# Scores of twelve heads as 64-row matmuls of two heads, and one scale transfer for each weight piece

## The reference

```python
x = x + xattn(layernorm(x), ctx)      # x: (2, 2048, 512), ctx: (2, 77, 512)
x = x + ffn(layernorm(x))             # 512 -> 1408 -> 512
# xattn: 16 heads of 32
q, k, v = heads(a @ Wq.T + bq), heads(ctx @ Wk.T + bk), heads(ctx @ Wv.T + bv)
s = einsum('bhtd,bhsd->bhts', q, k) / sqrt(32) + causal   # -inf above the diagonal
out = merge(einsum('bhts,bhsd->bhtd', softmax(s), v)) @ Wo.T + bo
# ffn: every operand rounded to fp4 in blocks of 16 along the last axis, with a scale per block
gate, y = fp4(x) @ fp4(w_gate).T, fp4(x) @ fp4(w_up).T
return fp4(silu(gate) * y) @ fp4(w_down).T
```

## Time and profile before

| | us |
|---|---|
| median of 3 runs | 1179.66 |
| lowest and highest run | 1179.59, 1182.97 |
| span of the profiled execution, first to last instruction | 1176.7 |
| PE busy | 1158.8 |
| VectorE busy | 970.3 |
| ScalarE busy | 483.5 |
| POOL busy | 179.3 |

### The profile page before, as it was taken

One profiled execution on the slowest core, in us unless ns is written; L12 is line 12 of the kernel. 1 busy time (PEld: TensorE's weight loads), 2 busy tenths in 40 slices (PEclk: granted clock), 3 DMA queues, 4 the chain that ended last, 5 costly groups with the idle time before them and its releaser, 6 DMA issues.

```text
span 1176.7 us, 21716 instructions
## 1 busy us (share of the span) xinstructions
PE 1158.8 (98%) x6784; PEld 1057.6 (90%) x6784; DVE 970.3 (82%) x1609; ACT 483.5 (41%) x1201; POOL 179.3 (15%) x305
## 2 busy tenths in 40 slices
PE   7899999999999999999999999999999999999998
PEld 6688888888888889999999999999999999999997
DVE  6778888888888877988888888888888888888865
ACT  3556656566566553333332332233233323333321
POOL 3433333333333310000000000000000000000000
PEclk9999999999999999999999999999999999999999
DMA  7223323323344436554445345444534454453442
GB/s 240 45 89 88 111 88 110 91 84 111 108 139 148 132 108 194 150 105 86 89 89 102 70 93 99 88 88 87 105 70 93 98 90 88 82 104 76 82 85 46
DMA packets 154955, 119.30 MB, mean 101 GB/s; under 512 B 95597, under 2 KB 122301, under 8 KB 154660
## 3 DMA queue, kind: packets, MB, share of 16 engines
q1 hardware_dynamic: 154916, 118.85, 42.7%
HBM read 74.47 MB, written 24.94 MB: 84 GB/s over the span
## 4 chain that ended last, share of the span: by engine, by line
PE 78%; SPq 7%; DMA 7%; DVE 2%; ACT 2%; issue 2%; POOL 2%; POOLq 0%; DVEq 0%; ACTq 0%
PE g_ps L175 7%; PE u_ps L175 7%; PE u_ps L176 7%; PE g_ps L176 7%; PE u_ps L177 7%; PE g_ps L177 7%; PE d_ps L1436 6%; PE d_ps L1437 6%; PE d_ps L1435 6%; SPq L504 4%; DMA ws_dram<-w_rows 4%; PE o_ps L784 3%; PE s_ps L764 3%; DMA w_wide<-ws_dram 3%; POOL w_q L586 2%
## 5 line engine op out<-in xcount | busy, mean ns | idle before, releaser
L175 PE MATMUL g_ps<-wguh,xnh 128*128 128x352 f32 x496 | 162.4, 327 | 0.5 <-issue 0.5
L175 PE MATMUL u_ps<-wguh,xnh 128*128 128x352 f32 x496 | 159.9, 322 | 0.5 <-DVE hid L1576 0.5
L176 PE MATMUL u_ps<-wgul,xnh 128*128 128x352 f32 x496 | 159.8, 322 | 0.0
L176 PE MATMUL g_ps<-wgul,xnh 128*128 128x352 f32 x496 | 159.8, 322 | 0.0
L177 PE MATMUL u_ps<-wguh,xnl 128*128 128x352 f32 x496 | 159.6, 322 | 0.0
L177 PE MATMUL g_ps<-wguh,xnl 128*128 128x352 f32 x496 | 159.5, 322 | 0.0
L898 ACT ACTIVATE probs<-s_ps,nsmax 128x77 f32<-128x77 f32 x512 | 113.7, 374 | 92.2 <-DVE nsmax L990 92.2
L1576 DVE TENSOR_TENSOR hid<-u_ps,silu 128x352 f32<-128x352 f32 x128 | 66.8, 522 | 78.1 <-PE u_ps L177 75.8
L1437 PE MATMUL d_ps<-wd,hql 128*128 128x512 f32 x330 | 128.9, 391 | 0.0
L1436 PE MATMUL d_ps<-wd,hqh 128*128 128x512 f32 x330 | 128.9, 391 | 0.0
L1435 PE MATMUL d_ps<-wd,hqh 128*128 128x512 f32 x330 | 128.4, 389 | 0.0
(11 more groups left out here) (175 smaller groups left out, 2547.1 us busy)
## 6 DMA issues: line engine op xcount, KB each, us to landing
scale_wide<-st_dram SPq DMA_DIRECT2D x248, 88.0 KB, 3.4
xin<-in_x_dram SPq DMA_DIRECT2D x32, 256.0 KB, 2.8
x_dram<-x SPq DMA_DIRECT2D x32, 256.0 KB, 2.2
xin<-x_dram SPq DMA_DIRECT2D x32, 256.0 KB, 2.7
out_dram<-y SPq DMA_DIRECT2D x32, 256.0 KB, 2.1
scale_wide<-st_dram SPq DMA_DIRECT2D x248, 32.0 KB, 1.8
w_wide<-ws_dram SPq DMA_DIRECT2D x240, 32.0 KB, 1.9
wd_dram<-wd_out SPq DMA_DIRECT2D x11, 512.0 KB, 3.0
```

What stands on the lines that cost most here:

```text
L175: pe.matmul(out, lh, rh, start=(i == 0), stop=False)
L176: pe.matmul(out, lh, rl, start=False, stop=False)
```

## The change

Heads 0 to 11 are computed two at a time. For each chunk `c` of 0 to 2 there are two calls: the lower 64 rows (heads 4c and 4c+1) write 154 columns of bank 0, the upper 64 rows (heads 4c+2 and 4c+3) write 154 columns of bank 1. Heads 12 to 15 stay one call of 128 rows into bank 2. So bank 0 holds heads 0, 1, 4, 5, 8, 9 and bank 1 holds 2, 3, 6, 7, 10, 11 (`S_ORDER`), and ScalarE writes each head's exponentials to its old place in `probs`. `s_done` for banks 0 and 1 is raised in the last round.

For the weight pieces, `grid_t` gets two buffers, and its transpose waits for POOL's product two pieces back. The scales lie in `ws_dram` as (8, 4, 128) instead of (4, 8, 128), and one DMA loads them to all 128 partitions. In SP's list the load of the next piece moves behind `scales_out` and `scales_in`.

```diff
+PAIR = 2 * CTX
-S_PARTS = [(0, 0, 4), (1, 4, 6), (1, 6, 8), (2, 8, 12), (3, 12, 16)]
+S_ORDER = [[4 * c + 2 * r + j for c in range(3) for j in range(2)] for r in range(2)] + [[12, 13, 14, 15]]
...
-        grid_t = sb("grid_t", [P, EC, P], BF16)
-        w_rows, w_wide = sb("w_rows", [E // BLK, P]), sb("w_wide", [P, EC, P])
+        grid_t = sb("grid_t", [P, 2, EC, P], BF16)
+        w_rows, w_wide = sb("w_rows", [E // BLK, P]), sb("w_wide", [P, EC * P])
...
             def scales_out(n):
                 sp.wait_ge(w_rows_ready, n - BY_DMA + 1)
                 if n > BY_DMA:
-                    sp.wait_ge(w_wide_loaded, 16 * (P // BLK) * (n - BY_DMA))
-                sp.dma_start(ws_dram.rearrange("c b k -> (c b) k"), w_rows[:]).then_inc(w_rows_stored, 16)
+                    sp.wait_ge(w_wide_loaded, 16 * (n - BY_DMA))
+                sp.dma_start(ws_dram.rearrange("b c k -> c b k"), w_rows[:]).then_inc(w_rows_stored, 16)
...
             def scales_in(n):
                 sp.wait_ge(w_rows_stored, 16 * (n - BY_DMA + 1))
                 if n > BY_DMA:
                     sp.wait_ge(wq_ready, n)
-                for b in range(P // BLK):
-                    sp.dma_start(w_wide[b * BLK:(b + 1) * BLK, :, :],
-                                 ws_dram[:, b, :].unsqueeze(0).to_broadcast([BLK, EC, P])).then_inc(w_wide_loaded, 16)
+                sp.dma_start(w_wide[:], ws_dram.rearrange("b c k -> b (c k)").unsqueeze(1).to_broadcast(
+                    [P // BLK, BLK, EC * P])).then_inc(w_wide_loaded, 16)
+
+            def grid_transposed(n):
+                sp.wait_ge(wquant.grid_ready, n + 1)
+                if n - 2 >= BY_DMA:
+                    sp.wait_ge(wq_ready, n - 1)
+                sp.dma_start_transpose(grid_t[:, n % 2], wquant.magic[:]).then_inc(grid_t_loaded, 16)
...
-                if n + 1 < PIECES:
-                    load_piece(n + 1)
                 if by_dma(n - 1):
                     scales_out(n - 1)
                     scales_in(n - 1)
+                if n + 1 < PIECES:
+                    load_piece(n + 1)
...
-                for i, (c, h0, h1) in enumerate(S_PARTS):
-                    bank, o = h0 // S_HEADS, (h0 % S_HEADS) * CTX
-                    out = s_ps[:, bank, o:o + (h1 - h0) * CTX]
+                def masked(out, heads):
                     if causal:
-                        pe.matmul(out, ident16[:], mask[:].unsqueeze(1).to_broadcast([P, h1 - h0, CTX]),
-                                  start=True, stop=False)
-                    last = pe.matmul(out, qt[:, c, :], kbd[:, b, c, (h0 % 4) * CTX:(h0 % 4 + h1 - h0) * CTX],
-                                     start=not causal, stop=True)
-                    if i in (1, 3, 4):
-                        last.then_inc(s_done, 1)
+                        pe.matmul(out, ident16[:], mask[:].unsqueeze(1).to_broadcast([P, heads, CTX]), start=True, stop=False)
+
+                for c in range(3):
+                    pairs = [s_ps[:, half, c * PAIR:(c + 1) * PAIR] for half in range(2)]
+                    for half in range(2):
+                        masked(pairs[half], 2)
+                    for half in range(2):
+                        r = slice(64 * half, 64 * (half + 1))
+                        last = pe.matmul(pairs[half], qt[r, c, :], kbd[r, b, c, half * PAIR:(half + 1) * PAIR],
+                                         start=not causal, stop=True)
+                        if c == 2:
+                            last.then_inc(s_done, 1)
+                masked(s_ps[:, 2, 0:4 * CTX], 4)
+                pe.matmul(s_ps[:, 2, 0:4 * CTX], qt[:, 3, :], kbd[:, b, 3, :],
+                          start=not causal, stop=True).then_inc(s_done, 1)
...
-    ws_dram = nc.dram_tensor("ws_dram", (EC, P // BLK, P), F32, kind="Internal").ap()
+    ws_dram = nc.dram_tensor("ws_dram", (P // BLK, EC, P), F32, kind="Internal").ap()
```

More of the change, by code:

```diff
@@ L583, in scale_turned @@
                 pool.wait_ge(grid_t_loaded, 16 * (n - BY_DMA + 1))
-                pool.wait_ge(w_wide_loaded, 16 * (P // BLK) * (n - BY_DMA + 1))
+                pool.wait_ge(w_wide_loaded, 16 * (n - BY_DMA + 1))
                 pool.wait_ge(wl_ready, n)
-                pool.tensor_tensor(w_q[:].rearrange("p (c k) -> p c k", k=P), grid_t[:], w_wide[:],
-                                   ALU.mult).then_inc(wq_ready, 1)
+                pool.tensor_tensor(w_q[:].rearrange("p (c k) -> p c k", k=P), grid_t[:, n % 2],
+                                   w_wide[:].rearrange("p (c k) -> p c k", k=P), ALU.mult).then_inc(wq_ready, 1)
             def iteration(a, n, down=None):
@@ L894, in exps @@
                     act.wait_ge(nsmax_ready, S_BANKS * t + bank + 1)
[L895 to L899, removed]
+                    for i, h in enumerate(S_ORDER[bank]):
+                        at = bank * S_HEADS + i
+                        last = act.activation(probs[:, h * CTX:(h + 1) * CTX], s_ps[:, bank, i * CTX:(i + 1) * CTX], ACT.Exp,
+                                              bias=nsmax[:, at:at + 1], scale=1.0)
                     last.then_inc(probs_ready, 1)
```

## The result

| | before | after |
|---|---|---|
| median of the runs | 1181.14 us (4 runs) | 1174.32 us (4 runs, 1171.94 to 1174.96) |
| span of the profiled execution | 1176.7 us | 1172.9 us |
| scores of tile 1 to scores of tile 31 | 371.02 us | 362.91 us |
| scores of tile 31 to the end | 757.6 us | 760.2 us |

The ratio is 0.9939 with a 95% interval of 0.9924 to 0.9954, so the changed kernel is about 7.2 us faster. 1174.1 us was forecast. The four rows above already tell that the agreement is not as clean as the number: the tiles in the third row gained 8.1 us where 6.2 were forecast for them (29 tiles of 0.24 us less, one masked tile of 0.8 us more), and the work behind them lost 2.6 us where nothing was.

What follows compares the result with a forecast made beforehand. PE was taken to bound attention, the weight loop close behind. Score savings of -7.2 us and +1.6 for masked tiles gave -5.6: span 1176.7 to 1171.1, plus 2.96 outside it, 1174.1 us; range 1159 to 1192.

Steps and rivals of the forecast that it cites:

- What bounds the kernel: Attention: PE sets the pace at 12.33 us a tile; the weight-piece loop, 12.45 us a piece, is close behind.
- Overlap: Six two-head score calls: the array's halves work fully side by side, 7 slots of 0.131 us, 0.92 us.
- rival 1: Score block: half-height loads go one after the other, block 2.25 us, total 1186.6 us, slower; chance 0.20.
- rival 2: Score block: no overlap at all, block 2.49 us, 1194 us, or 1180 with free shape changes; chance 0.15.
- Changes of shape: Entering and leaving the 64-row shape on PE costs 0.20 us each, twice a tile, 0.40 us.
- rival 4: Score block: changes of shape are free, total 1160 us; chance 0.52 shared with the forecast and its neighbours.
- Masked tiles: Tiles 0 and 16: three rounds, each entered and left, block 3.53 us, +0.8 us each, +1.6 for two.
- "No cost" for the path through the exponentials: From scores through exponentials to the probabilities' transposes: allows a tile every 11.2 us, under the 12.09 forecast, so no cost.
- The weight pieces: Weight loop: one scale load and a second buffer bring 12.45 to 10.0 us or less; worth nothing alone.
- Rival 3: Weight loop: single load lands late, loop stays 12.45 us, PE waits, about 1180 us; chance 0.08 with other no-change ways.
- The tail at 0: End of attention: PE's 1.3 us wait for VectorE's att stays; bounds 0 and -1.3 us, 0 taken.
- The sum: Whole kernel: -7.2 us for 30 tiles and +1.6 for the masked two make -5.6 us.

Runs made afterwards that it cites:

- the wait filled: Changed kernel plus 16 transposes that nobody reads, in PE's wait for VectorE's last attention results; 1171.26 us, ratio 0.9907.

## Why the prediction came out right

The mechanism and the sign were right; the number was helped by misses that cancel, and that it agrees to 0.2 us is luck. By the prediction's own steps:

- **What bounds the kernel.** Right. PE set the pace, and the weight loop, 0.12 us a tile slower, stood just behind: with the scores alone it came out at once (12.59 us a tile). "A granted clock of 2.4 GHz throughout" was wrong for the set-up (0.66 from 12 to 16 us); nothing in the sum hung on it.
- **Overlap.** Right in kind, mis-sized: "a call's second matmul waits for its first" gave seven slots, 0.92 us; measured are six pairs, 6 x 0.131 = 0.79 us. The two instructions of a call do not keep the halves apart; each half runs its own six in turn. The speedup table of the Trainium skill (TensorEngine Tiling (Array Packing), Theoretical Speedup), up to 2x for 64 rows, is met in full: 12 x 0.131 = 1.57 us became 0.79. The loads of the two halves run side by side as well (187 ns each, twelve of them within 0.82 us), which put an end to rival 1 and rival 2. The Trainium skill (TensorEngine Tiling (Array Packing), Key Properties) states that different tiles can execute loads and matmuls in parallel, and this trace agrees. (A 64-row load takes 187 ns, a 128-row one of the four-head call 189, as the Trainium skill's rule beside rival 1 had it; but since the loads of the halves run beside each other nothing is paid for that.)
- **Changes of shape.** Right: 0.40 us was taken, and the rows give 0.39. The distance from the projection's last matmul to the first score went from 0.23 to 0.32 us (0.09 of drain), the first pair's distance is 0.235 instead of 0.131 (0.104 of exposed load), and leaving the shape adds about 0.095 and 0.105. One row of the set-up and the idle-engine row had carried that. Together: 1.61 + 0.09 = 1.70 us, for 1.84 forecast. Two changes more cost 0.20 each again, so rival 4 is out.
- **Masked tiles.** Mis-sized: +0.8 us each was forecast, +0.07 measured. A round of masks and scores takes 0.71 us (231.70 to 232.41) where the prediction's parts make 0.95: two slots instead of three, and changes of shape that cost about 0.06 less each beside short mask matmuls.
- **"No cost" for the path through the exponentials.** This step failed. I took it as exponentials, transposes of the probabilities, 11.2 us a tile. The loop that counts goes on from the exponentials over four ScalarE steps to VectorE and takes 12.07 us; its rows were there in the trace of before, stretched to PE's 12.33 by slack too short to be marked (ScalarE's copy of q starts 0.36 us behind the scaled rows there, 0.15 in the changed kernel). At the forecast pace of 12.09 it would still have cost nothing; it cost because PE came out faster than forecast, at about 11.95. PE's own saving of 0.47 - 0.09 = 0.38 us a tile, 11.4 us over the 30 intervals from tile 1 to tile 31, shrank to 8.1, partly there (0.12 us a tile in tiles 3 to 15), partly in the tiles at the ends of the batches.
- **The weight pieces.** Right: worth nothing alone, needed for the rest. Rival 3 did not come: PE waits 0.2 us in all from 60 to 400 us. POOL's product moved from 2.1 to 5.4 us behind the start of the scores to about 2.3.
- **The tail at 0.** Mis-sized: bounds were 0 and -1.3, and it cost 2.6 us in the profiled execution, about 0.8 of it the collision on VectorE, 1.1 the clock, 0.7 a wait whose cause is open. The sentence "what is behind it on POOL comes earlier too" looked only at POOL; what the earlier product would stand beside on VectorE was not asked.
- **The sum.** -5.6 us was forecast. In the profiled execution the tiles gave -8.1, the tail +2.6 and the set-up +1.8: its span is 3.8 us shorter. The medians differ by 6.8 us, the ratio says 7.2. From tile 1 to tile 31 the forecast made -6.2 of its -5.6, so these tiles' gain was under-estimated by 1.9 us and the tail's loss by 2.6. The absolute number was helped once more: the forecast started from 1179.66 us for the kernel before, and with a fourth run its median became 1181.14, 1.5 us higher.

What stays open: how often the clock falls behind the last tile, and what decides it there; in all four runs with the wait filled the mean clock was 0.999 or more, and the wait's length alone does not tell. That the clock falls in the set-up of most profiled executions was seen and not tried, and PE's wait in the second feed-forward tile was not followed up.

## What to carry to other kernels

When one engine is busy 98% of the time, write down the second loop with every instruction that stands behind its last step, not only the data path: here it lay 0.3 us under the first, and shortening either loop alone gave under 2 us from tile 1 to tile 31 where both gave 10. Alternate the halves of the array call by call, and pay for a change of shape as seldom as possible: two more of them a tile cost more than the whole change had won. A transfer that becomes faster moves its consumer to another place; look at what runs beside it there, and at the gap that this opens on TensorE.

## What the runs showed of the hardware

- Matmuls of one row half can start before matmuls of the other half that stand ahead of them in the program: 299.787 us against 299.912, 300.043 and 300.174 in the kernel whose halves don't alternate. The Trainium skill (TensorE: Matmul & The Clock Gate, Part 3: Packing small matmuls — row/col tiling, The mechanism) states that matmuls start in program order; this trace differs.
- A VectorE operation on two tensors of SBUF took 1.54 us instead of 0.69 beside a POOL product that had started 0.24 us earlier: it ended 0.55 us after POOL did. The Trainium skill (SBUF — State Buffer, Who interferes with whom) states that a VectorE instruction with two inputs in SBUF contends with a GpSimd one that reads SBUF, and that issue order decides which of the two blocks; the trace agrees.
- TensorE's clock fell to its lower level of 1.2 GHz behind a wait of 1.7 us in one execution (0.65 on average from 420 to 424 us) and stayed at 1.00 behind waits of 1.7 and 2.0 us in two others.
